# Attention output squares transposed on TensorE and summed on VectorE, and the second feed-forward bias added by GpSimd

## The chip, the cores and the metric

The kernel runs on one core of one Trainium2 chip. The metric is the device time in microseconds, taken from outside the program; the profiler's span runs from the first to the last instruction. Engines are named as in the profile: PE is TensorE's matmul stream and PEld its weight loads, DVE is VectorE, ACT is ScalarE, POOL is GpSimd, SP is SyncE.

## What is computed

A language-model tower of depth one over 32 sequences of 512 byte tokens with width 128. Six n-gram rows are gathered for each token from a table, scaled and summed, joined with a byte embedding, and projected (the embedding part). Three layers follow, each with an attention part and a feed-forward part. Last comes a mixture of eight experts, of which each token takes one (the routing part and the expert stage). What the change touches is inside a layer (cut to that):

```python
for l in range(LAYERS):
    Y = _msr(_layernorm(X, ln1_w[l], ln1_b[l]), ...) + X
    Hn = _layernorm(Y, ln2_w[l], ln2_b[l])
    X = gelu(Hn @ ffn_w1[l] + ffn_b1[l]) @ ffn_w2[l] + ffn_b2[l] + Y
# inside _msr, Y is the attention output by head, 32 numbers a head:
m = Y.mean(-1, keepdims=True)
v = ((Y - m) ** 2).mean(-1, keepdims=True)
Yn = ((Y - m) / sqrt(v + EPS)) * gnw + gnb
```

## The kernel before

**Streams and rounds.** Two sequences (s = 0, 1) are in work at a time, each cut into two halves of 256 tokens (h = 0, 1). So four streams run side by side, and each goes through three layers of `attend` and `feed`. A pair of sequences is one round of 12 half-layers, and there are 16 rounds (`pairs`). Beside the layers of round `it` run the embedding of round it+1 and the routing of the round before. The 48 table gathers of a round are indirect DMAs whose descriptors POOL makes; they lie in POOL's queue between its arithmetic, as filler that is due a round later. After the last round follows the expert stage, which the change does not touch.

**Order.** Every engine has one queue in program order. That order is made when the program is built: each part of a stream is a generator that yields a due time before each of its steps, from the tables `AT` and `FIRST_AT` (lines 50 to 171; one number for each stream and layer) and the stream's start, and `by_progress` (line 548) always takes the step with the smallest due time. So a step's due time sets its place in its engine's queue, and nothing is moved at run time: an engine that waits holds everything behind it. `LATER_GATHERS` (line 33) does the same for the gathers.

**The attention output.** The matmuls of `attend` (PE, lines 1565 to 1575) leave y transposed in PSUM: 128 features on the partitions, 256 tokens along the free axis. ACT writes its squares to `sq` (line 890) and y times `gn_w` to `zp` (line 891). PE multiplies each 128-token chunk of `sq` with a 128x4 matrix of heads (lines 1576 to 1581), which gives for each token the sum of squares of its four heads: 128x8 for a half. DVE scales that by 1/32, adds EPS and writes `ms` (lines 1257 to 1260). POOL raises it to the power -0.5 (`gr`, line 795). ACT spreads `gr` over the 32 features of a head (`xn`, line 896), PE transposes that (line 1584, "pe rT_y"), and DVE multiplies it into `zp` (lines 1263 and 1264). PE's `o` projection and DVE's residual `Y1` (line 1268) end the part. The V weights are centred by head in the setup, so y has mean zero over a head.

**The norms.** ACT sums the squares of `Y1` (line 859), POOL raises the sum to the power -0.5 (`rstd`, line 771, "pool rstd2"), ACT multiplies `Y1` with it into `xn` (line 865, "act xn2"), which signals `n_out`, and PE transposes `xn` ("pe norm2_T", line 1497). The norm ahead of an attention part goes the same way from `X` ("pool rstd1"), with DVE multiplying (line 1166).

**The feed-forward bias.** In `feed` PE accumulates hidden times W2 in PSUM and then adds the second bias with two bf16 matmuls of 129 columns (lines 1618 and 1619): `three_bf` has ones in its first three rows, and `bias2` holds the bias split in three bf16 parts, made in the setup by `split_bias2` (lines 1115 to 1130). DVE then writes X = PSUM + `Y1` (line 1277), having waited for `ff_p` (the PSUM result) and `y1_s` (`Y1` written).

PE's helper `mm` is line 1471, so most matmuls have that line; the groups are told apart by their tensors ("moving,stationary": `con,sq` is the mean-square matmul, `bias,three_bf` the bias matmul, `con,xn` a transpose by the identity). An f32 matmul shows as two instructions, a transpose as one.

Of the kernel before, what the change touches and what calls it, by code (L numbers as in the profile page):

```python
# [8 lines left out]
BF16 = mybir.dt.bfloat16  # L9
I32 = mybir.dt.int32  # L10
U32 = mybir.dt.uint32
ALU = mybir.AluOpType
# [37 lines left out]
AT = {  # L50
# [60 lines left out]
FIRST_AT = {  # L111
# [76 lines left out]
def columns(widths):  # L188
# [11 lines left out]
    ("region", E), ("half", 16), ("tile", 80), ("gram_row", NG),  # L200
# [10 lines left out]
def constants(n_tokens):  # L211
# [31 lines left out]
    c[:, CONST["half"]] = -0.5  # L243
    c[:, CONST["tile"]] = np.arange(80)
# [4 lines left out]
def tower_program(nc, x, gram_table, layer_w, params, consts, expert_w, out):  # L249
# [13 lines left out]
    with ExitStack() as ctx:  # L263
        def sb(name, shape, dt=F32):
            return ctx.enter_context(nc.sbuf_tensor(name, shape, dt))
# [4 lines left out]
        def two(make, name, *a):  # L270
            return [make(f"{name}{s}", *a) for s in range(2)]
# [25 lines left out]
        def param(name, k=None, width=1):  # L297
            a = par[:, PARAM[name]]
            return a if k is None else a[:, k * width:(k + 1) * width]
# [18 lines left out]
        bias2 = sb("bias2", [P, LAYERS * WIDE], BF16)  # L318
        bias2_part = [sb(f"bias2_part{n}", [P, LAYERS * WIDE], BF16) for n in range(3)]
        bias2_rest = sb("bias2_rest", [P, LAYERS * WIDE])  # L320
        three_bf = sb("three_bf", [P, P], BF16)
        below_three = sb("below_three", [P, 1])
# [93 lines left out]
        def chunks(ap):  # L416
            return ap.rearrange("p (c n) -> p c n", c=CH)
# [52 lines left out]
        y1_s = two(sem, "attention_residual_ready")  # L470
        f_p = two(sem, "ffn_hidden_in_psum")
# [135 lines left out]
        def bank_a(s, h):  # L607
            return bank(s, 2 * h)
# [82 lines left out]
        def _(pool):  # L691
# [76 lines left out]
            def norm_rstd(it, s, k, h):  # L768

                pool.wait_ge(n_ss[s][h], nth(it, OWN, k))  # L770
                pool.tensor_tensor(rstd[s][:, CS[h]], ss[s][:, CS[h]], const("half")[:, 0:2], ALU.pow)\  # L771
                    .then_inc(n_rstd[s][h], 1)
# [24 lines left out]
            def feed(it, s, l, h):  # L797
                yield at("pool rstd2", it, s, h, l)
                norm_rstd(it, s, 2 * l, h)

# [33 lines left out]
        def _(act):  # L834
# [38 lines left out]
            def attend(it, s, l, h):  # L873
# [16 lines left out]
                act.activation(sq[s][:, CS[h], :], chunks(bank_a(s, h))[:, 0:2, :], ACT.Square)  # L890
# [99 lines left out]
        def _(dve):  # L990
# [124 lines left out]
            def split_bias2():  # L1115

                rest = param("ffn_b2")
                for n in range(3):
                    link(dve.tensor_copy(bias2_part[n][:, :], rest))
                    if n < 2:  # L1120
                        link(dve.tensor_tensor(bias2_rest[:, :], rest, bias2_part[n][:, :], ALU.subtract))
                        rest = bias2_rest[:, :]
                link(dve.tensor_scalar(bias2[:, :], bias2_part[0][:, :], eye[:, 0:1], None, ALU.mult))
                for n in (1, 2):
                    link(dve.scalar_tensor_tensor(bias2[:, :], bias2_part[n][:, :], eye[:, n:n + 1], bias2[:, :],
                                                  ALU.mult, ALU.add))
                link(dve.tensor_scalar(below_three[:, :], const("vocab"), 3.0, None, ALU.is_lt))
                dve.tensor_scalar(three_bf[:, :], ones_bf[:, :], below_three[:, :], None, ALU.mult)

            split_bias2()  # L1130
# [84 lines left out]
            def attend(it, s, l, h):  # L1215
# [34 lines left out]
                for m in range(2):  # L1250
# [8 lines left out]
                dve.tensor_scalar(ms[s][:, h * n:(h + 1) * n], a[:, 2 * P:2 * P + n], 1.0 / HD, EPS, ALU.mult, ALU.add)\  # L1259
                   .then_inc(y_ms[s], 1)  # L1260
# [10 lines left out]
            def feed(it, s, l, h):  # L1271
                k = it * LAYERS + l
                cs = CS[h]
                yield at("dve x", it, s, h, l)
                dve.wait_ge(ff_p[s], nth(k, 2, h))
                dve.wait_ge(y1_s[s], nth(k, 2, h))
                dve.tensor_tensor(X[s][:, cs, 0:WIDE], wide(bank_a(s, h)), Y1[s][:, cs, 0:WIDE], ALU.add).then_inc(x_s[s], 1)
# [191 lines left out]
        def _(pe):  # L1469
# [50 lines left out]
            def attend(it, s, l, h):  # L1520
# [57 lines left out]
                for c in half_chunks(h):  # L1578
                    last = mm(a[:, 2 * P + c % 2 * HEADS:2 * P + (c % 2 + 1) * HEADS], sq[s][:, c, :],
                              const("heads").rearrange("p (n d) -> p n d", d=HD)[:, :, 0])  # L1580
                last.then_inc(ms_p[s], 1)
# [9 lines left out]
            def feed(it, s, l, h):  # L1591
# [20 lines left out]
                for f in range(FB):  # L1612
                    if f % 2 == 0:
                        yield at(f"pe w2_{f // 2}", it, s, h, l)
                        pe.wait_ge(f_s[s], nth(k, 4, 2 * h + f // 2))
                    for i in range(2):
                        mm(wide(a)[:, i, :], hid[s][:, h, f, chunk(i)], w2[:, f, :], f == 0 and i == 0, False)
                for i in range(2):
                    last = mm(wide(a)[:, i, :], three_bf[:, :], bias2[:, l * WIDE:(l + 1) * WIDE], False, i == 1)
# [135 lines left out]
```

## Time and profile before

| what | us |
|---|---|
| runs: median of 3 (lowest, highest) | 2427.72 (2426.78, 2428.72) |
| the profiled execution's own time | 2428.14 |
| its span | 2426.3 |
| PE busy over the span | 2233.4 (92%) |
| PEld busy | 1950.1 (80%) |
| DVE busy | 1887.8 (78%) |
| POOL busy | 1764.3 (73%) |
| ACT busy | 1580.5 (65%) |

The own time is 1.8 us above the span (what lies around the first and last instruction) and 0.4 us above the median of the runs. The span has three stretches: a head of some 100 us, in which the tables are loaded, hashed and gathered; the 16 rounds, to about 2200 us; and the expert stage. Busy shares are averages over all three, so a stage is read from windows and from the timeline. PE's matmuls overlap in the records; what one costs in a full queue is the distance between starts, not its duration. POOL's queue shows gaps of 0.2 to 0.3 us ahead of each indirect DMA (put down to "issue"), in which it isn't free either.

### The profile page before, as it was taken

How to read it: one execution, taken by the hardware profiler on the slowest of the kernel's cores; microseconds unless marked ns; L12 is line 12 of the kernel's file. 1: busy time of each engine (PE TensorE's matmuls, PEld its weight loads, DVE VectorE, ACT ScalarE, POOL GpSimd, SP SyncE). 2: the span in 40 equal slices, each digit the busy share in tenths (PEclk: the TensorE clock that was granted, in tenths of full speed). 3: DMA queues.
4: the chain of work that ended last, by engine and by line, in shares of the span. 5: the costliest groups of instructions: out<-in, count | busy, mean ns of one | idle time of the engine just before them, and what ended most of it. 6: DMA issues, size and time to landing. Idle time of an engine off the chain costs nothing.

```text
span 2426.3 us, 52865 instructions
## 1 busy us (share of the span) xinstructions
PE 2233.4 (92%) x18308; PEld 1950.1 (80%) x18309; DVE 1887.8 (78%) x5669; ACT 1580.5 (65%) x5066; POOL 1764.3 (73%) x1762
## 2 busy tenths in 40 slices
PE   1489999999999999999999999999999999986985
PEld 0368888888888888888888888888888888875874
DVE  5757878888787888888888888887878888766653
ACT  0256677776767676776776777767676777763653
POOL 5687777777777777777787777777777774333777
PEclk9789999999999999999999999999999999997997
DMA  3111111111111111111111111111111111002332
GB/s 122 28 45 34 24 41 28 40 29 41 27 40 28 36 32 37 33 35 37 26 43 26 42 27 40 29 41 27 37 30 37 33 28 55 2 8 75 101 103 69
DMA packets 63522, 98.11 MB, mean 40 GB/s; under 512 B 19108, under 2 KB 41126, under 8 KB 63152
## 3 DMA queue, kind: packets, MB, share of 16 engines
q0 software_dynamic: 33216, 67.44, 10.6%
q1 hardware_dynamic: 30064, 27.53, 4.1%
q8 instruction: 141, 2.31, 0.4%
q14 instruction: 101, 0.83, 0.1%
HBM read 76.63 MB, written 19.17 MB: 39 GB/s over the span
## 4 chain that ended last, share of the span: by engine, by line
PE 75%; POOL 9%; DVE 8%; issue 4%; ACT 3%; DMA 0%; DVEq 0%; POOLq 0%; SPq 0%
PE psum L1471 65%; PE psum L1492 7%; POOL both_grams L760 4%; PE psum L1545 3%; POOL gr L795 3%; POOL out L821 3%; DVE hid L1254 2%; ACT qm L885 1%; ACT qkT L883 1%; ACT xn L896 1%; DVE side_n L1205 1%; DVE qk L1233 0%; DVE hid L1230 0%; DVE qk L1229 0%; POOL rstd L771 0%
## 5 line engine op out<-in xcount | busy, mean ns | idle before, releaser
L760 POOL DMA_INDIRECT both_grams<-gram_table,idx_all x768 | 780.3, 1016 | 188.5 <-issue 183.0
L1471 PE MATMUL psum<-xT,lw 128*128 128x256 f32 x1920 | 481.8, 385 | 0.0
L795 POOL TENSOR_TENSOR gr<-ms,con 128x8 f32<-128x8 f32 x192 | 319.1, 1662 | 137.9 <-DVE ms L1259 133.1
L1471 PE MATMUL psum<-lw,hid 128*128 128x129 f32 x3072 | 391.0, 276 | 3.4 <-ACT hid L915 3.4
L1471 PEld LDWEIGHTS psum<-lw,hid 128*128 128x128 f32 x3072 | 370.9, 192 | 12.9 <-issue 5.6
L771 POOL TENSOR_TENSOR rstd<-ss,con 128x2 f32<-128x2 f32 x320 | 233.9, 733 | 195.1 <-ACT squares L859 192.7
L1471 PEld LDWEIGHTS psum<-xT,lw 128*128 128x128 f32 x1920 | 341.2, 192 | 32.5
L915 ACT ACTIVATE hid<-psum,par 128x256 f32<-128x256 f32 x768 | 307.1, 486 | 43.8 <-PE psum L1471 41.1
L1471 PE MATMUL psum<-lw,xT 128*128 128x256 f32 (+1 forms) x1536 | 287.9, 330 | 6.5 <-ACT xT L871 6.5
L871 ACT ACTIVATE xT<-psum,par 128x256 f32<-128x256 f32 x384 | 213.5, 560 | 119.8 <-PE psum L1492 118.8
L1471 PEld LDWEIGHTS psum<-lw,xT 128*128 128x128 f32 x1536 | 250.0, 192 | 33.0 <-ACT xT L871 7.2
L1254 DVE TENSOR_TENSOR hid<-psum,con 128x512 f32<-128x512 f32 x384 | 249.5, 684 | 27.2 <-PE psum L1471 23.9
L1492 PE MATMUL psum<-con,xn 128*128 128x128 f32 x1152 | 238.5, 289 | 32.0 <-ACT xn L896 16.4
L1471 PE MATMUL psum<-qm,qkT 64*128 64x256 f32 x1536 | 219.7, 405 | 28.9 <-ACT qm L885 17.2
L1492 PEld LDWEIGHTS psum<-con,xn 128*128 128x128 f32 x1152 | 130.6, 147 | 91.8 <-issue 27.1
L865 ACT ACTIVATE xn<-Y,rstd 128x128 f32<-128x128 f32 x384 | 133.0, 396 | 102.1 <-POOL rstd L771 102.1
L883 ACT ACTIVATE qkT<-psum 128x512 f32<-128x512 f32 x192 | 114.5, 596 | 108.9 <-PE psum L1545 107.2
L1471 PEld LDWEIGHTS psum<-qm,qkT 64*128 64x128 f32 x1536 | 133.3, 187 | 64.0 <-ACT qm L885 23.4
L1229 DVE TENSOR_TENSOR qk<-psum,con 128x512 f32<-128x512 f32 x192 | 131.6, 685 | 65.8 <-PE psum L1471 65.7
L859 ACT ACTIVATE squares<-Y 128x129 f32<-128x129 f32 x384 | 116.1, 308 | 97.1 <-DVE Y L1268 97.1
L1205 DVE SCALAR_TENSOR_TENSOR side_n<-both_grams,gate,side_n 128x256 f32<-128x256 f32 x320 | 157.2, 491 | 8.1
L885 ACT ACTIVATE qm<-psum,con 128x256 f32<-128x256 f32 x384 | 160.8, 477 | 0.0
(244 smaller groups left out, 4747.6 us busy)
## 6 DMA issues: line engine op xcount, KB each, us to landing
both_grams<-gram_table,idx_all POOLq DMA_INDIRECT x768
xb<-x SPq DMA_DIRECT2D x32, 256.0 KB, 3.3
idx_all<-routed_rows SPq DMA_DIRECT2D x20, 132.0 KB
er<-routed_rows SPq DMA_DIRECT2D x20, 132.0 KB
both_grams<-routed_rows SPq DMA_DIRECT2D x20, 132.0 KB
qm<-routed_rows SPq DMA_DIRECT2D x20, 132.0 KB
both_grams<-expert_w SPq DMA_DIRECT2D x8, 321.0 KB, 5.2
lw<-layer_w SPq DMA_DIRECT2D x1, 2503.5 KB, 11.9
```

Source lines behind the costliest of these rows:

```text
L760: pool.indirect_dma_start(grams[s][:, g, c, :], None, gram_table, bass.IndirectOffsetOnAxis(ap=idx_all[:, g, at:at + 1], axis=0))\
L771: pool.tensor_tensor(rstd[s][:, CS[h]], ss[s][:, CS[h]], const("half")[:, 0:2], ALU.pow)\
L795: pool.tensor_tensor(gr[s][:, c], ms[s][:, c], const("half")[:, 0:n], ALU.pow).then_inc(y_r[s], 1)
L865: last = act.activation(xn[s][:, c, :], src[s][:, c, 1:WIDE], ACT.Copy, scale=scale[s][:, c:c + 1])
L871: act.activation(xT[s][:, TS[h]], src[:, 0:2 * P], ACT.Identity, bias=b, scale=w).then_inc(xT_s[s][h], 1)
L883: act.activation(qkT[s][:, h].rearrange("p a c n -> p (a c n)"), bank_b(s, h), ACT.Copy)
L885: last = act.activation(qm[s][:, h, j, :], bank_b(s, h)[:, 0:2 * P], ACT.Copy, scale=const("parity")[:, j:j + 1])
L915: last = act.activation(hid[s][:, h, 2 * m + f, :], src[:, f * 2 * P:(f + 1) * 2 * P], ACT.Gelu, bias=param("ffn_b1", l * FB + 2 * m + f))
L1205: last = dve.scalar_tensor_tensor(acc, grams[s][:, g, CS[h], :], gate[:, g:g + 1], acc, ALU.mult, ALU.add)
L1254: dve.tensor_tensor(A[s][:, h, m], chunks((a, b)[m]), causal.unsqueeze(1).to_broadcast([P, HEADS, P]), ALU.mult).then_inc(sc_s[s], 1)
L1471: return pe.matmul(dst, lhsT, rhs, start=start, stop=stop)
L1492: last = pe.transpose(dst[:, (c % 2) * P:(c % 2 + 1) * P], src[:, c, :], eye)
```

## The change

It has two parts. **The squares.** ACT's square takes a scale of 32^-0.5 and a bias of (EPS/32)^0.5, a new constant column, so that the sum of 32 squares is the mean square plus EPS (the cross term vanishes, since y has mean zero over a head). PE transposes the two chunks of `sq` into 256 PSUM columns where it had multiplied them with the heads, and DVE sums them by head, 32 at a time, with a `tensor_reduce` of 128x256 to 128x8 where it had scaled 128x8. **The bias.** The two bf16 matmuls of each half-layer go, and with them the setup that splits the bias. POOL adds the f32 bias to `Y1` in place, 128x258 numbers, in a step of its own, "pool bias", due at 7.2 us in `feed` for every stream and layer. It waits for `n_out` (ACT has read `Y1` for the norm), and DVE's X waits for the semaphore `y1_b` of that step in place of `y1_s`.

```diff
 AT = {
+    "pool bias": ((7.2, 7.2, 7.2), (7.2, 7.2, 7.2), (7.2, 7.2, 7.2), (7.2, 7.2, 7.2)),
...
 FIRST_AT = {
+    "pool bias": ((7.2, 7.2, 7.2), (7.2, 7.2, 7.2), (7.2, 7.2, 7.2), (7.2, 7.2, 7.2)),
...
-    ("region", E), ("half", 16), ("tile", 80), ("gram_row", NG),
+    ("region", E), ("half", 16), ("root_eps", 1), ("tile", 80), ("gram_row", NG),
...
+    c[:, CONST["root_eps"]] = (EPS / HD) ** 0.5
...
-        bias2 = sb("bias2", [P, LAYERS * WIDE], BF16)
...
             def feed(it, s, l, h):
                 yield at("pool rstd2", it, s, h, l)
                 norm_rstd(it, s, 2 * l, h)
+                yield at("pool bias", it, s, h, l)
+                pool.wait_ge(n_out[s][h], nth(it, NORMS, 2 * l + 1))
+                pool.tensor_tensor(Y1[s][:, CS[h], 0:WIDE], Y1[s][:, CS[h], 0:WIDE],
+                                   param("ffn_b2", l, WIDE).unsqueeze(1).to_broadcast([P, 2, WIDE]), ALU.add)\
+                    .then_inc(y1_b[s], 1)
...
-                act.activation(sq[s][:, CS[h], :], chunks(bank_a(s, h))[:, 0:2, :], ACT.Square)
+                act.activation(sq[s][:, CS[h], :], chunks(bank_a(s, h))[:, 0:2, :], ACT.Square,
+                               bias=const("root_eps"), scale=float(HD) ** -0.5)
...
-            def split_bias2():
...
-            split_bias2()
...
-                dve.tensor_scalar(ms[s][:, h * n:(h + 1) * n], a[:, 2 * P:2 * P + n], 1.0 / HD, EPS, ALU.mult, ALU.add)\
-                   .then_inc(y_ms[s], 1)
+                dve.tensor_reduce(ms[s][:, h * n:(h + 1) * n], a[:, 2 * P:].rearrange("p (n d) -> p n d", d=HD),
+                                  axis=AX_X, op=ALU.add).then_inc(y_ms[s], 1)
...
-                dve.wait_ge(y1_s[s], nth(k, 2, h))
+                dve.wait_ge(y1_b[s], nth(k, 2, h))
...
-                for c in half_chunks(h):
-                    last = mm(a[:, 2 * P + c % 2 * HEADS:2 * P + (c % 2 + 1) * HEADS], sq[s][:, c, :],
-                              const("heads").rearrange("p (n d) -> p n d", d=HD)[:, :, 0])
-                last.then_inc(ms_p[s], 1)
+                half_transposes(a[:, 2 * P:], sq[s], h).then_inc(ms_p[s], 1)
...
-                        mm(wide(a)[:, i, :], hid[s][:, h, f, chunk(i)], w2[:, f, :], f == 0 and i == 0, False)
-                for i in range(2):
-                    last = mm(wide(a)[:, i, :], three_bf[:, :], bias2[:, l * WIDE:(l + 1) * WIDE], False, i == 1)
+                        last = mm(wide(a)[:, i, :], hid[s][:, h, f, chunk(i)], w2[:, f, :], f == 0 and i == 0,
+                                  f == FB - 1 and i == 1)
                 last.then_inc(ff_p[s], 1)
```

## Rows read from the trace of the kernel before

**Rows 1.** the page, part 4, whole span: engines on the chain that ended last

```profile
PE 75%; POOL 9%; DVE 8%; issue 4%; ACT 3%; DMA 0%; DVEq 0%; POOLq 0%; SPq 0%
```

**Rows 2.** windows, 900 to 1300 us: length, then busy us per engine, PE clock, DMA

```profile
900.00:1300.00 400.00, 395.43 (x3342) 345.96 (x3341) 331.75 (x988) 284.50 (x932) 311.69 (x311) 1.00 0.13 34
```

**Rows 3.** POOL timeline, one round apart: start, us, instruction, [idle before]

```profile
942.58 1.65 POOL L795 TENSOR_TENSOR gr<-ms,con 128x8 f32<-128x8 f32 x1
...
1071.74 1.65 POOL L795 TENSOR_TENSOR gr<-ms,con 128x8 f32<-128x8 f32 x1
```

**Rows 4.** groups by line and form, whole span: count, busy us, mean ns, idle

```profile
L1259 DVE TENSOR_SCALAR ms<-psum 128x8 f32<-128x8 f32 x192 | 31.9, 166 | 40.8 <-PE psum L1471 40.8
...
L1263 DVE TENSOR_TENSOR zp<-psum,zp 128x256 f32<-128x256 f32 x192 | 80.5, 419 | 28.1 <-PE psum L1492 26.2
```

**Rows 5.** PE timeline, two stretches of a middle round

```profile
910.31 0.50 PE L1471 MATMUL psum<-con,sq 128*128 128x4 f32 x4
910.68 0.41 PE L1492 MATMUL psum<-con,xn 128*128 128x128 f32 x2
...
919.64 0.28 PE L1471 MATMUL psum<-bias,three_bf 128*128 128x129 bf16 x2
919.76 0.39 PE L1492 MATMUL psum<-con,xn 128*128 128x128 f32 x2
919.98 0.51 PE L1471 MATMUL psum<-par,side_T 128*128 128x8 f32 x4
```

**Rows 6.** DVE timeline, setup

```profile
28.32 0.29 DVE L1109 TENSOR_REDUCE lw<-lw 128x1 f32<-128x128 f32 x1
...
29.16 0.69 DVE L1109 TENSOR_REDUCE lw<-lw 128x4 f32<-128x512 f32 x1
...
35.73 0.35 DVE L1201 TENSOR_SCALAR side_n<-both_grams,gate 128x256 f32<-128x256 f32 x1 [3.87 <-DMA both_grams<-gram_table,idx_all]
```

**Rows 7.** POOL timeline, setup: one integer sum of 48 and one of 720 numbers

```profile
14.15 0.28 POOL L719 TENSOR_TENSOR hid<-hid 128x48 int32<-128x48 int32 x1
...
87.40 1.70 POOL L719 TENSOR_TENSOR rest_limb<-rest_limb,qm 128x720 int32<-128x720 int32 x1
```

**Rows 8.** DVE timeline at 87 us, and line 1205: ns min/median/max

```profile
87.51 4.22 DVE L1205 SCALAR_TENSOR_TENSOR side_n<-both_grams,gate,side_n 128x256 f32<-128x256 f32 x3
...
L1205 DVE SCALAR_TENSOR_TENSOR side_n<-both_grams,gate,side_n x320: 468/485/1862, 36.1 to 2021.9; 128x256 f32<-128x256 f32 x160
```

**Rows 9.** waits of POOL, 500 to 1800 us: us in total, times, longest

```profile
POOL rstd L771 <- ACT squares L859: 82.2, 128, 1.5
...
POOL gr L795 <- DVE ms L1259: 63.8, 51, 1.9
```

**Rows 10.** POOL timeline of a middle round, four of its chained powers

```profile
907.90 0.70 POOL L771 TENSOR_TENSOR rstd<-ss,con 128x2 f32<-128x2 f32 x1 [0.57 <-ACT squares L859]
...
911.20 1.69 POOL L795 TENSOR_TENSOR gr<-ms,con 128x8 f32<-128x8 f32 x1
...
919.75 0.86 POOL L771 TENSOR_TENSOR rstd<-ss,con 128x2 f32<-128x2 f32 x1 [0.38 <-ACT squares L859]
...
951.91 0.73 POOL L771 TENSOR_TENSOR rstd<-ss,con 128x2 f32<-128x2 f32 x1
```

**Rows 11.** ACT timeline, the normalisation after the power at 919.75

```profile
920.64 0.69 ACT L865 ACTIVATE xn<-Y,rstd 128x128 f32<-128x128 f32 x2 [0.98 <-POOL rstd L771]
```

**Rows 12.** PE timeline, transposes that those results feed, and the scores behind

```profile
921.49 0.44 PE L1492 MATMUL psum<-con,xn 128*128 128x128 f32 x2
...
944.83 0.38 PE L1492 MATMUL psum<-con,xn 128*128 128x128 f32 x2
...
945.94 1.14 PE L1471 MATMUL psum<-qm,qkT 64*128 64x256 f32 x8 [0.29 <-ACT qm L885]
...
953.50 0.38 PE L1492 MATMUL psum<-con,xn 128*128 128x128 f32 x2
```

**Rows 13.** chain of waits, 100 to 240 us (the first round): shares by line

```profile
by line: POOL both_grams L760 31.6%; PE psum L1471 25.4%; issue 10.0%; POOL gr L795 7.4%; POOL rstd L771 5.2%; PE psum L1492 3.2%; PE psum L1545 1.3%; DVE X L1182 1.1%; ACT hid L915 1.1%; DVE lw L1111 1.0%; DVE hid L1254 0.9%; ACT L915 0.9%
```

More of the change, by code:

```diff
@@ L317, in tower_program @@
         Y1 = two(sb, "Y1", [P, CH, WIDE + 1])
-        bias2 = sb("bias2", [P, LAYERS * WIDE], BF16)
[L319 to L322, printed above, removed]
         xn = two(sb, "xn", [P, CH, H])
@@ L470, in tower_program @@
         y1_s = two(sem, "attention_residual_ready")
+        y1_b = two(sem, "attention_residual_with_bias_ready")
         f_p = two(sem, "ffn_hidden_in_psum")
@@ L1113, in _ @@
             centred(param("ffn_b2").rearrange("p (l n) -> p l n", l=LAYERS))
-            def split_bias2():
[L1117 to L1128, printed above, removed]
-            split_bias2()
             for s in range(2):
```

## The prediction

> **What bounds the kernel now.** I read the chain of waits first: PE holds 75% of it, POOL 9%, DVE 8% [rows 1]. Then a window in the middle: of 400 us PE is busy 395, at granted clock 1.00 (the 2.4 GHz level), DVE 332, POOL 312 [rows 2]. The timeline repeats itself: the same `gr` starts at 942.58 and at 1071.74, so a round is 129.2 us [rows 3], and 14 of the 16 rounds are alike. PE's queue is full; its starts follow each other without gaps. But the other queues are close behind. POOL waits on semaphores only 82.2 + 63.8 = 146 us in 1300 us, ten rounds, so 14.5 us a round [rows 9]; in the other 114.7 it works or issues DMAs. Where PE's next input comes from POOL's power (`rstd`, `gr`), its margin is small, and that decides this change.
>
> **PE, removed and added.** The mean-square group starts at 910.31 and the next at 910.68: 0.37. A pair of transposes takes 919.76 to 919.98: 0.22. The two bias matmuls take 919.64 to 919.76: 0.12 [rows 5]. So PE saves 0.15 + 0.12 = 0.27 in each of the 192 half-layers, 3.2 us a round, 52 us in all. Were PE the only limit, 2428 would become 2376, and no edit here can give more.
>
> A transpose takes 0.11 for 128 columns [rows 5] in a stretch at clock 1.00 [rows 2], with hundreds of transposes in it. The Trainium skill (TensorE: Matmul & The Clock Gate, Part 4: PE-mode transpose) says that transposes do not bring the clock to its full rate. By that rule a pair would cost an estimated 0.44, PE would lose 0.07 instead of gaining 0.15, and the sum below would end some 20 us higher. The rows here speak against it, and it gets no chance.
>
> **DVE.** `ms` takes 0.17 on 8 numbers; a DVE operation that reads 256 PSUM numbers takes 0.42 [rows 4]. Sums of 128 and 512 numbers take 0.29 and 0.69 [rows 6], which puts 256 at 0.42 too. Bounds 0.29 and 0.69; I take 0.42. That is 0.25 more per half-layer, 3.0 a round, on an engine that is busy 83% [rows 2]. On the path from PE's squares to `gr` it is 0.25 - 0.15 = +0.1. ACT's square with a scale and a bias keeps its shape; I cost it at nothing, since ACT has a quarter of its time free [rows 2].
>
> **POOL's new step.** No f32 sum on POOL is in the trace. The nearest are integer sums: 0.28 for 48 numbers and 1.70 for 720 [rows 7]; a line through them gives 0.72 for 258. Bounds: 0.28 (all fixed cost) and 1.70; in practice 0.4 to 0.85. I take 0.72. It adds 12 x 0.72 = 8.6 us a round against 14.5 of waiting, so POOL still fits into a round (about 123 of 126 to 129), but with most of its slack gone. What counts is where in the queue it falls. I merged the due times of the tables as the program does:
>
> Place 1: two bias steps fall between the power at 907.90 and the one at 919.75, the first right behind 907.90, the second one step behind `gr` at 911.20. POOL waited only 0.38 ahead of 919.75 [rows 10], so that power comes 2 x 0.72 - 0.38 = 1.06 late. ACT normalises from 920.64 for 0.69 [rows 11] and PE's transposes start at 921.49 [rows 12], 0.16 after it; some 0.1 of that is spare. PE stalls about 0.95.
> Place 2: a bias step falls directly ahead of the power at 951.91, which already followed POOL's queue without a wait [rows 10]. It ends 0.86 before PE's transposes at 953.50 [rows 12], and the same normalisation lies between. PE stalls 0.66.
> Place 3: a bias step falls one gather ahead of `gr` at 942.58, which had no wait ahead of it [rows 3]. It ends at 944.23, its transposes start at 944.83, and the scores at 945.94 waited 0.29 for ACT [rows 12], which works behind the spreading of `gr`. PE stalls 0.72.
> The other eight fall ahead of waits that take them, or of results whose margin is larger. With the +0.1 of the sums at some three `gr` that start when `ms` arrives, a round gains stalls of 0.95 + 0.66 + 0.72 + 0.3 = 2.6.
>
> Against that stands PE's saving, but where PE waits for such a result, what it saved since it fed that path is lost in the wait. By the same merging some 4 bias groups and 6 squares groups of a round lie in such stretches: 4 x 0.12 + 6 x 0.15 = 1.4. So 3.2 - 1.4 = 1.8 is kept, and a round grows by 2.6 - 1.8 = 0.8.
>
> **Waits and setup.** POOL's wait for `n_out` holds its queue, but the norm is applied some 2 us or more before the bias is reached, so it costs nothing; DVE's X is due at 10.68 at the earliest against 7.2 for the bias, so `y1_b` comes about 3 us ahead, and if that cover went, X and the next layer of that stream would be late by what is missing. No DMA moves to another queue, but every gather behind a bias step is issued later; they are due a round ahead, which hides it. The setup that goes (ten DVE steps before 28 us) lies ahead of a 3.87 us wait of DVE for the first gathers [rows 6]: nothing gained.
>
> **The sum.** 14 rounds x 0.8 = +11. In the first round POOL itself is the chain: gathers 31.6, `gr` 7.4, `rstd` 5.2, issue 10.0, together 54% [rows 13]; 12 x 0.72 x 0.54 = +4.7. In the last round there are no gathers, POOL has room, and PE keeps 3.2 - 0.6 = -2.6. Together +13 on the profiled execution's own 2428.14 (0.4 above the median of the runs): 2441 us.
>
> **Rivals.** A, faster: POOL's add is short. With its duration d the stalls of the three places are 4d - 0.54; against 1.8 - 0.3 kept they break even at d = 0.51. At d = 0.28, the fixed cost of the row, they are 0.6, and about half of the lost savings come back (0.6): a round shrinks by 1.5, 14 x 1.5 + 2.6 - 2 = 22, so 2406; with all savings kept some 2390. For it: PE's full queue and its 75% of the chain. Against it: the slope of the integer sums. The case d = 0.45 to 0.6 is the one of no change.
> B, slower still: POOL's add holds up DVE. While the sum of 720 ran on POOL (87.40 for 1.70 [rows 7]), three DVE operations with two SBUF inputs took 4.22 us, where the median of one is 0.485 and the longest took 1.862 [rows 8], so DVE stood until POOL's sum was done. The Trainium skill (SBUF — State Buffer, SBUF: two separate sides) says that the two engines share one port pair that is locked for a whole instruction; the trace agrees. Here, a DVE operation that meets a bias step would stand for half of it on average, 0.36. If half of the 12 meet one in a stretch where DVE has no wait to give, that is 2.2 a round, 14 x 2.2 = 30, and 2471; if all do, 2500. Against it: DVE still has 17% free, and the small powers of POOL show no such stand.
>
> **Chances.** Forecast (POOL late at three places, 2441, by itself 2433 to 2458) 0.40; B (2471) 0.20; A (2390 to 2422) 0.27; no change 0.13. A measurement of this kernel can tell about 0.2%, 5 us. That gives faster 0.27, same 0.13, slower 0.60. The range must reach into A and B: 2395 leaves out the end of A, 2488 the end of B, together under 2 in 10.
>
> **What would show it.** Right: mean-square transposes 0.22 apart, no bias matmuls, `ms` near 0.42, POOL's new add near 0.72; a round of about 130; POOL's waits for ACT's squares and DVE's `ms` down from 14.5 to some 6 a round; PE waits for ACT's normalisation at the three places. Wrong: an add under 0.5 with rounds below 129 (A); DVE operations with two SBUF inputs far above their medians and PE waiting for DVE (B); X waiting for the bias, which I cost at nothing; or new waits at other places, since the margins come from one order of events.

## The result and the profile after

The changed kernel takes 2506.33 us (median of 5 runs, 2504.79 to 2507.31), the kernel before 2427.72 beside it: a ratio of 1.0324, interval 1.0313 to 1.0336, 78.6 us slower. The prediction was 2441 with a range to 2488: the side was right, the size was not.

First the chain that ended last, part 4 of the page of the kernel after (shares of the span, by engine, then by line):

```profile
POOL 42%; DVE 25%; PE 19%; issue 10%; ACT 4%; DMA 0%; DVEq 0%; POOLq 0%; SPq 0%
PE psum L1460 16%; POOL both_grams L759 15%; POOL gr L794 9%; POOL rstd L770 5%; POOL routed_rows L812 5%; DVE hid L1243 4%; POOL Y L801 3%; POOL out L825 2%; DVE qk L1222 2%; PE psum L1481 2%; ACT squares L863 2%; DVE hid L1219 2%; DVE qk L1218 2%; DVE side_n L1194 1%; DVE ms L1248 1%
```

Before, PE held 75% of it [rows 1]; now POOL does most, and the new add itself (L801) is only 3%. Another engine has become the bound, and not by the new step alone: by all that stands in the same queue. The window of [rows 2], after (busy us of each engine, granted clock):

```profile
900.00:1300.00 400.00, 376.83 (x3069) 318.88 (x3068) 337.85 (x950) 273.96 (x890) 326.61 (x333) 1.00 0.12 33
```

PE went from 395 to 377 of 400 at the same clock of 1.00, POOL from 312 to 327. The round, from the timeline of POOL after (start, duration): the same bias add one round apart.

```profile
903.73 0.90 POOL L801 TENSOR_TENSOR Y<-Y,par 128x258 f32<-128x258 f32 x1
...
1038.83 0.91 POOL L801 TENSOR_TENSOR Y<-Y,par 128x258 f32<-128x258 f32 x1
```

135.1 us, against 129.2 [rows 3]. 14 rounds of 5.9 would be 83 us, a little over the 78.6, since some rounds after take 134.7; so nearly all of the loss is in the steady rounds. The terms of the sum, from the instructions grouped by form after (busy us, mean ns, idle time before them); the first row is of the whole span, the other two of 500 to 1800 us:

```profile
L801 POOL TENSOR_TENSOR Y<-Y,par 128x258 f32<-128x258 f32 x192 | 144.9, 755 | 3.2 <-ACT xn L869 0.8
...
L1248 DVE TENSOR_REDUCE ms<-psum 128x8 f32<-128x256 f32 x116 | 48.3, 417 | 9.0 <-PE psum L1481 9.0
...
L894 ACT ACTIVATE sq<-psum,con 128x256 f32<-128x256 f32 x116 | 54.2, 468 | 13.2 <-PE psum L1460 12.7
```

and a pair of mean-square transposes with what follows it, in the timeline of PE after:

```profile
896.25 0.38 PE L1481 MATMUL psum<-con,sq 128*128 128x128 f32 x2
896.50 1.99 PE L1460 MATMUL psum<-xT,lw 128*128 128x256 f32 x8
```

The add (0.755 against 0.72 taken), the sum (0.417 against 0.42) and the pair (0.25 here, against 0.22) came out near the terms; the square, costed at nothing, takes 468 ns where it took 378. The add waited 0.8 us for `n_out` in the whole run. Now the waits from 500 to 1800 us after (us in total, times, longest); 1300 us are 9.6 rounds:

```profile
ACT xn L901 <- POOL gr L794: 66.0, 87, 1.4
...
POOL gr L794 <- DVE ms L1248: 58.7, 59, 2.4
...
POOL rstd L770 <- ACT squares L863: 50.2, 88, 1.5
DVE xn L1155 <- POOL rstd L770: 43.3, 47, 1.4
...
PE psum L1481 <- ACT xn L901: 23.7, 38, 0.9
...
DVE X L1171 <- POOL side_mom L775: 19.5, 20, 1.7
...
PE psum L1481 <- ACT xn L869: 18.8, 29, 1.2
...
DVE xn L1155 <- POOL rstd L783: 13.4, 10, 1.4
PE psum L1534 <- DVE qk L1222: 13.3, 29, 0.6
```

and of before, all waits of DVE for POOL's powers and all waits of PE (10.1 rounds):

```profile
DVE xn L1166 <- POOL rstd L771: 24.2, 30, 1.2
...
PE psum L1471 <- ACT qm L885: 10.4, 20, 0.7
...
DVE X L1182 <- POOL side_mom L776: 2.6, 10, 0.3
...
PE psum L1471 <- DVE hid L1254: 2.2, 10, 0.2
```

POOL still waits 109 us, 11.3 a round, where it waited 14.5 [rows 9]. So of the 9.1 us that 12 adds bring to a round only 3.2 went into its waits, and the other 5.9 are the growth of the round. DVE waits 76 us for powers of POOL, 7.9 a round, where it waited 26.8 us, 2.7 a round. These waits stand in DVE's queue, ahead of work for all four streams. Nothing waited for the add itself or for a gather in that stretch.

PE's matmuls (the weight loads, PEld, not counted) waited 12.6 us before, 1.3 a round, and never for `xn`. After, all its waits come to 69.8 us, 7.3 a round. The three places of the prediction are among them, in the timeline of PE after (place 1, 3 and 2):

```profile
953.31 0.44 PE L1481 MATMUL psum<-con,xn 128*128 128x128 f32 x2 [1.21 <-ACT xn L869]
...
977.83 0.44 PE L1481 MATMUL psum<-con,xn 128*128 128x128 f32 x2 [0.93 <-ACT xn L901]
...
987.07 0.44 PE L1481 MATMUL psum<-con,xn 128*128 128x128 f32 x2 [0.45 <-ACT xn L869]
```

They are 2.6 us together, against 0.95 + 0.66 + 0.72 = 2.3 forecast. The other 3.4 us a round that were added stand where the sum has no price but 0.3 for the squares' sums, such as 0.81 for `xn` at 934.96 and 0.60 for DVE's rotary sum at 915.94. A stretch of the chain after, in order of time (start, us, what), shows how POOL's lateness travels through DVE's queue:

```profile
910.67 0.74 POOL side_mom L775
911.41 0.03 issue
911.44 0.04 DVE X L1171
...
915.20 0.69 DVE qk L1222
915.89 0.33 DVE sw L1226
916.22 0.34 DVE ms L1248
916.57 0.07 issue
916.63 1.63 POOL gr L794
...
1005.89 1.67 POOL gr L794
...
1027.77 0.72 POOL rstd L770
```

and the waits in it, from the timelines: first the same X of DVE before, then X and `gr` after.

```profile
880.50 0.67 DVE L1182 TENSOR_SCALAR X<-h,side_mom 128x128 f32<-128x128 f32 x2 [0.26 <-POOL side_mom L776]
...
911.44 0.66 DVE L1171 TENSOR_SCALAR X<-h,side_mom 128x128 f32<-128x128 f32 x2 [1.71 <-POOL side_mom L775]
...
916.63 1.63 POOL L794 TENSOR_TENSOR gr<-ms,con 128x8 f32<-128x8 f32 x1 [0.16 <-DVE ms L1248]
```

Here the waiting runs in a loop. POOL comes late to a power, behind two of the new adds; DVE's X (of the side stream) waits 1.71 us for it at the head of DVE's queue, where it waited 0.26; the DVE operations behind it start late one after the other, the last of them is `ms`, and POOL, late as it is, still waits for that `ms` at `gr`. Such a wait is no room: it moves with POOL. How many of POOL's waits are of this kind no view adds up; e5 and e13 measure it from outside. From 1005.89 to 1027.77 POOL works and issues without one wait.

### The profile page after: what moved, and what is told of

It is laid out like the page before. It is cut to its first block, busy times and chain, and to the rows that moved or that the text cites. A ratio compares the mean times of both kernels' runs of the same rounds, so it can differ in the third digit from the quotient of the medians.

```text
span 2504.9 us, 51511 instructions
## 1 busy us (share of the span) xinstructions
PE 2223.9 (89%) x17540; PEld 1888.7 (75%) x17541; DVE 1972.8 (79%) x5659; ACT 1595.9 (64%) x5066; POOL 1914.7 (76%) x1954
## 4 chain that ended last, share of the span: by engine, by line
POOL 42%; DVE 25%; PE 19%; issue 10%; ACT 4%; DMA 0%; DVEq 0%; POOLq 0%; SPq 0%
PE psum L1460 16%; POOL both_grams L759 15%; POOL gr L794 9%; POOL rstd L770 5%; POOL routed_rows L812 5%; DVE hid L1243 4%; POOL Y L801 3%; POOL out L825 2%; DVE qk L1222 2%; PE psum L1481 2%; ACT squares L863 2%; DVE hid L1219 2%; DVE qk L1218 2%; DVE side_n L1194 1%; DVE ms L1248 1%
## 5 line engine op out<-in xcount | busy, mean ns | idle before, releaser
L759 POOL DMA_INDIRECT both_grams<-gram_table,idx_all x768 | 789.6, 1028 | 178.9 <-issue 173.6
L1481 PEld LDWEIGHTS psum<-con,xn 128*128 128x128 f32 x1152 | 128.3, 144 | 188.9 <-ACT xn L901 78.3
L812 POOL DMA_INDIRECT routed_rows<-row,slot x128 | 137.5, 1074 | 36.4 <-issue 32.9
```

Of the source, the lines that this page charges most:

```text
L759: pool.indirect_dma_start(grams[s][:, g, c, :], None, gram_table, bass.IndirectOffsetOnAxis(ap=idx_all[:, g, at:at + 1], axis=0))\
L812: pool.indirect_dma_start(slots, bass.IndirectOffsetOnAxis(ap=slot[s][:, c:c + 1], axis=0), row[s][:, c, :], None).then_inc(r_done[s], 16)
L1481: last = pe.transpose(dst[:, (c % 2) * P:(c % 2 + 1) * P], src[:, c, :], eye)
```

## The experiments

Theory Q: GpSimd's queue lost the time. Rivals: VectorE's longer sums (D), the add holding VectorE up by its memory access (L), and others that each expectation names. The kernel before took 2427.2 to 2427.9 beside each group of runs, so times of different groups can be set against each other. The first four runs split the change.

**e1, the squares alone**

```diff
-  act.activation(sq, y, ACT.Square)
+  act.activation(sq, y, ACT.Square, bias=const("root_eps"), scale=HD ** -0.5)
-  dve.tensor_scalar(ms, a[:, 2P:2P+n], 1/HD, EPS, mult, add)
+  dve.tensor_reduce(ms, a[:, 2P:] by heads, add)
-  mm(..., sq, const("heads")) twice
+  half_transposes(a[:, 2P:], sq, h)
```

> Only the squares part is made; the bias stays on PE. Theory Q (POOL's new step in its queue is the whole cost): PE saves 0.15 in each half-layer, DVE's sum is 0.25 longer but covered, so 2400 to 2430 us. Theory D (the longer path from the squares to the power: DVE 0.17 to 0.42, ACT 0.38 to 0.47) : at least 50 of the 79 us, 2475 or more. Theory X (neither alone, the two parts take each other's slack): 2430 to 2455.

Measured 2432.32, ratio 1.0020 (1.0011 to 1.0029): a small loss, just past Q's range, inside that of X, and far from D.

**e2, the bias alone** (the rest of the diff: GpSimd's add, no bias matmuls)

> Only the bias part is made; the squares go through the matmul with the heads as before. Theory Q: most of the 79 us, 2480 to 2510. Theory D: 2415 to 2440, since PE loses 0.12 of work in each half-layer and POOL has room. Theory X: 2435 to 2460, less than half of the loss.

2505.72, ratio 1.0324 (1.0310 to 1.0338): the whole loss, within 0.6 us of the full change. It lies in Q's range; D and X fall.

**e3, squares with the bias left out altogether**, and **e4, the kernel before with the bias left out**

```diff
-  pool.tensor_tensor(Y1, Y1, ffn_b2, add).then_inc(y1_b)      # and no bias matmuls
-  dve.wait_ge(y1_b)
+  dve.wait_ge(y1_s)
```

> The changed kernel without POOL's step; the second feed-forward bias is left out of the computation altogether, so PE has neither its matmuls nor POOL its sum. Theory Q: PE's whole saving of up to 52 us shows, 2380 to 2405. Theory D: still slower than before, 2450 or more. Theory X: between 2405 and 2440.

> The kernel before without its two bias matmuls; the second feed-forward bias is left out of the computation. It prices the PE work alone: 192 x 0.12 = 23 us if PE is the only limit, 2405; near 2427 if other queues take it up. All three theories expect 2405 to 2420; Theory X expects the upper end.

2418.46 (0.9965, 0.9952 to 0.9978) and 2413.36 (0.9944, 0.9929 to 0.9960). e4 lies in the range that all had, e3 above Q's, in that of X: TensorE's whole saving did not show, and here Q was wrong. Taking the bias off TensorE is worth 14 of the 23 us that 192 x 0.12 make, and the squares cost 5 us with or without it. GpSimd's step costs 2505.7 - 2413.4 = 92 us for 144 us of work. All later costs are counted from e4.

**e5, a power of the same length in place of the add; bias left out**

```diff
-  pool.tensor_tensor(Y1, Y1, ffn_b2, add).then_inc(y1_b)
+  pool.tensor_tensor(spare, const("rank")[:, 0:2], const("half")[:, 0:2], pow).then_inc(y1_b)
```

> The squares as in the kernel before; GpSimd's step stands at its place, waits and signals as in the bias-only kernel, but it is a power of 128x2 values from constants into a scratch tile, so it has nearly the duration of the add (the other 128x2 powers take 0.70 to 0.74 us, the add 0.755) and touches 4 columns of a partition instead of 774. The second feed-forward bias is left out of the result. Theory Q (GpSimd's queue is the resource: each step of 0.7 us makes the powers behind it late, and VectorE and ScalarE wait in order for those): what counts is the duration, so 2485 to 2510 us, nearly the 2505.7 of the bias-only kernel. Rival L (the add and VectorE hold each other up when both read and write wide tiles): the power takes that away, so at most half of the 92 us stays, 2413 to 2460. Rival W (VectorE's sum waits for GpSimd's signal): that needs only the place and the signal, as Q, but then VectorE's X would show idle time behind this step.

2481.19, ratio 1.0220 (1.0206 to 1.0234), 67.8 over e4: between the two, much nearer to Q. A step that reads 4 numbers a partition and helps nobody costs 73% of what the add costs, by standing in the queue. W falls, since no instruction waited for the step. For the other 24 us the groups by form of DVE, 500 to 1800 us, first of e5:

```profile
L1252 DVE SCALAR_TENSOR_TENSOR zp<-zp,par,sw 128x256 f32<-128x256 f32 x116 | 57.3, 494 | 4.1
...
L1337 DVE TENSOR_TENSOR pick_bf<-picked,top 128x16 bf16<-128x16 f32 x40 | 7.7, 193 | 1.4
```

then of e2, with the add:

```profile
L1252 DVE SCALAR_TENSOR_TENSOR zp<-zp,par,sw 128x256 f32<-128x256 f32 x115 | 65.1, 566 | 4.1
...
L1337 DVE TENSOR_TENSOR pick_bf<-picked,top 128x16 bf16<-128x16 f32 x39 | 12.8, 328 | 1.3
```

The same instructions are longer with the add: 566 against 494 ns, 328 against 193. Of the 115 `zp` in e2, the 28 that ran beside an add took 526 to 1056 ns, 806 on average, and the others 489. About 4 of the 24 us are due to length, since the add takes 749 ns and this power 731 (at the 200 us for each us that e13 gives). By the window 900 to 1300, DVE's busy time times the round over 400 is 107 us a round before, in e4 and in e5, and 111 in e2.

**e6, half of the add; the other chunk's bias left out**

```diff
+  first = slice(2 * h, 2 * h + 1)
-  pool.tensor_tensor(Y1[:, CS[h]], Y1[:, CS[h]], ffn_b2 twice, add)
+  pool.tensor_tensor(Y1[:, first], Y1[:, first], ffn_b2, add)
```

> As the bias-only kernel, but GpSimd adds the bias to the first of a half's two token chunks alone (128x129 values instead of 128x258), at the same place and with the same wait and signal; the other chunk's bias is left out of the result. It should take some 0.4 to 0.5 us instead of 0.755. The kernel without the step takes 2413.4 us and the one with it 2505.7. Theory Q with a queue that is full at this place: the cost follows the step's whole length on GpSimd, so 92 x (0.4 to 0.5)/0.755 = 49 to 61, 2460 to 2475 us. Rival S (GpSimd has some slack a round, and the cost starts when that is used up): less than in proportion, 2420 to 2450. Rival F (the step costs by being there, a wait and a signal in the queue, not by its length): over 2480.

2455.11, ratio 1.0112 (1.0096 to 1.0127), 41.7 over e4 for a step of 451 ns: between Q and S, F falls.

**e7, the same add at other places in GpSimd's queue**

```diff
- "pool bias": ((7.2, 7.2, 7.2), (7.2, 7.2, 7.2), (7.2, 7.2, 7.2), (7.2, 7.2, 7.2)),
+ "pool bias": ((7.2, 4.4, 10.4), (3.95, 8.25, 11.85), (7.2, 7.2, 10.95), (4.0, 7.2, 5.15)),
```

> The bias-only kernel with nothing changed but due times of GpSimd's step: of a round's 12 steps 8 are put directly ahead of a power at which GpSimd waited in the trace of the kernel without the step (for the mean squares from VectorE or the sums from ScalarE, 0.27 to 1.72 us each, 6.6 us in all), the other 4 stay. The result is complete. Theory Q: what lies in a wait costs nothing, so the part of the 8 steps beyond their waits (about 1.2 us a round) and the 4 others (3 us) are left of 9 us a round: a third to a half of the 92, 2440 to 2465 us. Rival L (the add holds VectorE up by its reads and writes wherever it stands): 2490 to 2510. Rival C (a wait of GpSimd is closed by the time that it was itself late earlier, so a step in it only moves it): 2475 to 2500.

2470.13, ratio 1.0175 (1.0161 to 1.0189). It lies between Q and C: 36 of the 92 us are had back by places alone, but 57 stay. The waits of POOL in e7, 500 to 1800 us:

```profile
POOL rstd L770 <- ACT squares L863: 39.4, 59, 1.5
POOL gr L794 <- DVE ms L1247: 33.7, 33, 2.1
...
POOL Y L801 <- ACT xn L869: 8.0, 10, 0.8
```

That is 8.3 us in each of 9.8 rounds, where e2 has 11.4 and e4, without the step, 13.7: at these places 5.4 us of waiting were filled, at the old ones 2.3. So the places count. What the 57 us are made of this run does not tell. Four steps were not moved, and 14 rounds of 4 x 0.73 are 41 us if each costs its length; one moved step waits 0.8 us a round for `n_out`; and the add still holds VectorE up. That a step in a wait of the loop costs something is therefore not shown here.

**e8, the squares-only kernel without scale and bias operand; both left out of the result**

```diff
-  act.activation(sq, y, ACT.Square, bias=const("root_eps"), scale=HD ** -0.5)
+  act.activation(sq, y, ACT.Square)
```

> The squares-only kernel (bias by TensorE as before, squares transposed and summed by VectorE), but ScalarE's square has no scale and no bias operand, as in the kernel before: the division by the head size and the epsilon are left out of the result. ScalarE's square should take 378 ns again instead of 469. The squares-only kernel takes 2432.3 us, 5 above before, and I had expected a gain of some tens of us. Theory A (ScalarE's 0.09 us a half-layer, on the way from the attention output to the powers, took part of the gain): 192 x 0.09 = 17 us at most, 2415 to 2427 us. Rival V (VectorE's sum, 0.25 us longer than the copy that it replaces and on the same way, took it): 2430 to 2434, no change. Rival N (TensorE's saving was never on the way): also no change.

2429.84, ratio 1.0009 (1.0000 to 1.0018), with the square back at 378 ns: 2.5 us less than e1, which is less than the 0.2% that a measurement can tell, so 0.09 us in each of 192 steps counts for little. A falls; N and V are left.

**e9, the squares-only kernel with half of the sum; the other half of the squares left out**

```diff
-  dve.tensor_reduce(ms, a[:, 2P:] by heads, add)
+  dve.tensor_reduce(ms, (a[:, 2P:] by heads)[:, :, 0:HD // 2], add)
```

> The squares-only kernel, but VectorE's sum takes the first half of each head's values alone (128x128 read instead of 128x256); the other half of the squares is left out of the result. VectorE's sum should take about 0.29 us (as its other 128x128 from PSUM) instead of 0.42. The squares-only kernel takes 2432.3 us. Theory V (VectorE's longer step on the way from the attention output to GpSimd's power is what takes the gain of TensorE): half of the 0.25 us more goes, 192 x 0.13 = 25 us at most, 2410 to 2425. Rival N (VectorE has idle time here and TensorE's saving was never on the way, so neither counts): 2428 to 2434.

2421.66, ratio 0.9974 (0.9964 to 0.9985). The group of the sum in e9, 500 to 1800 us:

```profile
L1261 DVE TENSOR_REDUCE ms<-psum 128x8 f32<-128x128 f32 x121 | 34.7, 287 | 14.4 <-PE psum L1494 14.0
```

0.13 us less per sum gave 10.6 of 25 us: V, and N falls. VectorE's longer step is what the squares part pays, and TensorE's 0.15 does not outweigh it. Whether it pays on the way to `gr` or by holding the rest of VectorE's queue, this run does not separate.

**e10, a shorter power in the kernel before; the powers of six of a half's eight values left out**

```diff
-  pool.tensor_tensor(gr[8 columns], ms[8 columns], const("half")[:, 0:8], pow)
+  pool.tensor_tensor(gr[2 columns], ms[2 columns], const("half")[:, 0:2], pow)
-  act.activation(xn by heads, gr[8 columns] spread over 32 each, Copy)
+  act.activation(xn, gr[2 columns] spread over 128 each, Copy)
```

> The kernel before, but GpSimd's power of the mean squares takes 2 of a half's 8 values a partition (128x2 instead of 128x8), and ScalarE spreads these two over all heads; the powers of the other heads are left out of the result. This step should take 0.72 us instead of 1.69, 0.97 less, 12 times a round. The runs so far gave 92.6 us for each 1 us that was put into GpSimd's queue per half-layer step (power instead of the add: 67.8 for 0.731; half add: 41.7 for 0.451). Theory Q2 (GpSimd's queue already sets the round in the kernel before, and the cost is a straight line through it): the same slope downwards, 0.97 x 92.6 = 90 us less, 2335 to 2350 us. Rival K (TensorE sets the round before, as 395 of 400 us busy say, and the queue's cost only begins there: a knee at about the time of the kernel without the bias): 2410 to 2427 us. Rival M (shorter latency helps in part): 2370 to 2405.

2415.65, ratio 0.9947 (0.9933 to 0.9960). The row of e10 in the window 900 to 1300:

```profile
900.00:1300.00 400.00, 396.16 (x3355) 347.44 (x3348) 331.55 (x986) 284.58 (x932) 279.15 (x312) 1.00 0.13 34
```

K, and Q2 and M fall: GpSimd lost 33 of 312 us and the kernel 12 us in all. PE stayed at 396 of 400. Before the change the queue did not set the round.

**e11, the same add on VectorE**

```diff
-  pool.wait_ge(n_out); pool.tensor_tensor(Y1, Y1, ffn_b2, add).then_inc(y1_b)
+  dve.wait_ge(n_out);  link(dve.tensor_tensor(Y1, Y1, ffn_b2, add))
```

> The bias-only kernel with the same in-place add at the same due time, issued by VectorE instead of GpSimd, with no signal to wait for at X. The result is complete. VectorE is busy for 107 of a round's 128.3 us without the step; its other 128x258 adds take 0.42 us, so 5 us a round more. Theory Q (it is GpSimd's queue that is short of time, not VectorE's): VectorE has room, and a step costs its length where something waits behind it, at the 0.48 that GpSimd's showed or less: 192 x 0.42 x 0.48 = 39 us over the kernel without the step, 2425 to 2455 us. Rival V (VectorE has in-order waits of its own and every us counts in full): 2413 + 81, 2485 to 2500 us. Rival F (VectorE's step is free, as it lies in its idle time): 2411 to 2420 us, faster than before.

2431.15, ratio 1.0014 (1.0005 to 1.0023): 18 us over e4, in Q's range, where GpSimd's step costs 92. Its group and the chain of e11:

```profile
L1258 DVE TENSOR_TENSOR Y<-Y,par 128x258 f32<-128x258 f32 x192 | 80.4, 419 | 0.0
```

```profile
PE 61%; DVE 21%; POOL 9%; issue 6%; ACT 2%; DMA 0%; DVEq 0%; POOLq 0%; SPq 0%
```

VectorE is busier than GpSimd by the busy row, and still had the room: its 80 us of work cost 18, it adds nothing to GpSimd's queue with the 44 powers and 56 DMA issues of a round, and PE stays on the chain.

**e12, the bias matmuls of the kernel before as one**

```diff
-  for i in range(2): mm(wide(a)[:, i, :], three_bf, bias2[l], False, i == 1)
+  mm(wide(a), three_bf, bias2[l] twice, False, True)
```

> The kernel before, but TensorE adds the bias to a half's two chunks by one multiplication of 258 columns instead of two of 129. The result is complete. In the trace of the kernel before the pair takes 0.12 us from its start to the next start at a clock of 1.00 (0.06 each). If TensorE pays by columns alone: no change, within 0.2% of before. If each instruction has a cost of its own that the neighbours don't hide: up to 0.03 us less each, 192 x 0.03 = 6 us at most, 2421 to 2426.

2424.93, ratio 0.9990 (0.9981 to 0.9999). The timeline of PE in e12:

```profile
906.24 0.27 PE L1471 MATMUL psum<-bias,three_bf 128*128 128x258 bf16 x1
906.35 0.38 PE L1492 MATMUL psum<-con,xn 128*128 128x128 f32 x2
```

0.11 to the next start instead of 0.12 [rows 5]. It is the fastest version with a complete result, by less than the 0.2% that a measurement can tell, so the two theories are not told apart.

**e13, a still shorter power in the queue; bias left out**

```diff
-  pool.tensor_tensor(spare[2 columns], const("rank")[:, 0:2], const("half")[:, 0:2], pow)
+  pool.tensor_tensor(spare[1 column], const("rank")[:, 0:1], const("half")[:, 0:1], pow)
```

> The kernel with a power in place of the add, but the power takes 1 value a partition instead of 2 (128x1). The second feed-forward bias is left out of the result. The powers of 128x2 and 128x8 took 0.73 and 1.70 us, 0.16 for each value more, so this one should take about 0.57. The same place, wait and signal. Straight line (the queue's cost starts with the first ns: 67.8 us for 0.731): 0.57 x 92.7 = 53 us over the 2413.4 of the kernel without the step, 2463 to 2470. Slack first (the half add's 41.7 hold some 10 us of hold-up of VectorE, so the queue's part is 31 for 0.451 and 68 for 0.731, 130 us for each us behind a slack of 0.2): 47 us, 2456 to 2462. Present at all (the step costs by its being there): over 2475.

2455.20, ratio 1.0113 (1.0097 to 1.0130), 41.8 over e4. The groups of the two powers, e13 first:

```profile
L802 POOL TENSOR_TENSOR spare<-con 128x1 f32<-128x1 f32 x192 | 115.3, 601 | 3.2 <-ACT xn L869 0.8
```

```profile
L802 POOL TENSOR_TENSOR spare<-con 128x2 f32<-128x2 f32 x192 | 140.4, 731 | 3.1 <-ACT xn L869 0.8
```

The duration was 0.601, not 0.57, and the time is still below both ranges: the line is steeper than either theory had it. 0.13 us more in each of 192 steps cost 26 us, and 192 x 0.13 is 25: between these two lengths the queue's time counts in full. Followed down, the cost ends at 0.601 - 41.8/200 = 0.39 us a step, 4.7 us a round. An estimate from two points, but the waits of POOL from 500 to 1800 us bear it out, in e4:

```profile
POOL rstd L769 <- ACT squares L857: 74.2, 119, 1.5
POOL gr L793 <- DVE ms L1241: 64.4, 53, 2.0
```

and in e5:

```profile
POOL rstd L771 <- ACT squares L863: 53.1, 89, 1.5
POOL gr L795 <- DVE ms L1247: 37.6, 40, 2.1
```

138.6 us in 10.1 rounds of 128.3 are 13.7 a round; 90.7 in 9.8 rounds of 133.2 are 9.3. So at these places 4.4 us a round were filled, and 9.3 stayed although the rounds grew by 4.9.

**e14, e7 with the power in place of the add; bias left out**

```diff
- "pool bias": ((7.2, 7.2, 7.2), (7.2, 7.2, 7.2), (7.2, 7.2, 7.2), (7.2, 7.2, 7.2)),
+ "pool bias": ((7.2, 4.4, 10.4), (3.95, 8.25, 11.85), (7.2, 7.2, 10.95), (4.0, 7.2, 5.15)),
-  pool.tensor_tensor(Y1, Y1, ffn_b2, add).then_inc(y1_b)
+  pool.tensor_tensor(spare, const("rank")[:, 0:2], const("half")[:, 0:2], pow).then_inc(y1_b)
```

> The kernel with the steps moved ahead of GpSimd's waits, with the power of 128x2 constants in place of the add; the second feed-forward bias is left out of the result. With the add the moved steps gave 2470.1 us, 57 over the kernel without the step. Hold-up (the add stops VectorE when both want wide tiles): VectorE's busy time a round was 2.4 us longer with the moved add than with a power, against 3.9 for the add at its first place, which cost 24 us more than the power; so 24 x 2.4/3.9 = 15 us less, 2450 to 2460 us. No hold-up (the 24 came from the order of events of that one pair): 2466 to 2472. Moving alone decides (what stands in a wait is free): the 4 steps that stay and what sticks out of the waits, some 25 us, 2435 to 2445.

2457.88, ratio 1.0125 (1.0108 to 1.0142): 12.3 us below e7, 44.5 over e4, in the range of the hold-up, although the power took longer here (777 ns against 728 for the moved add). So the hold-up shows in a second pair, 12 us beside the 24. Moving alone falls (2435 to 2445).

## Why the prediction was right or wrong

**The account.** From e2, e4 and e5: +68 for the time in GpSimd's queue, +24 for what only the add does, -14 for the bias matmuls, +78 together, and the full change is 0.6 us above that. The squares cost 5 us alone and nothing measurable beside the bias, since PE is then no longer the bound.

**PE's saving.** Its size was right, its worth was not. The bias matmuls gave 14 of 23 us (e4), about the share that I let PE keep. The squares gave less than nothing (e1), because VectorE's step between the attention output and `gr` became longer (e9). I had that as 0.25 - 0.15 = +0.1 at some three `gr`, and it was more: half of the sum's growth is worth 10.6 us (e9). The square's 0.09, costed at nothing "since ACT has a quarter of its time free", lies on the same way, but e8 gives it 2.5 us, within what a measurement can tell.

**The failed step** is "The other eight fall ahead of waits that take them, or of results whose margin is larger", and with it the sum of 2.6 us of stalls and the round of +0.8. The three stalls that were priced came: 2.6 us, against 2.3. But PE's waits grew by 6.0 us a round, so 3.4 us stand where the sum has 0.3 and the other eight steps were to cost nothing; and since the round grew by 5.9, next to nothing of the 1.8 us that PE was to keep is seen. Two things broke the step. First, POOL's 14.5 us of waiting [rows 9] were taken as room for 8.6. In the changed kernel they shrank by 3.2, and the power in place of the add filled 4.4 (e5). The chain after shows why for one of them: it is a wait for DVE, which had itself waited for POOL. That most of the rest are of this kind is inferred from their staying, not shown one by one, and the room depends on the places (5.4 in e7). Second, I followed POOL's lateness to PE at the powers' direct users only, with everything else left where it was, and not into DVE's queue, where `xn` and the side stream's X wait in order for powers, 7.9 us a round after, with the masks, the rotary products and `ms` behind them. "POOL still fits into a round" was the wrong test: a queue with some 4.5 us to give at these places was given 9.

**Rival A** fell on its own condition: the add took 0.755, over the 0.51 of the break-even.

**Rival B**, the add holding up DVE, was real but was the smaller part: 24 us of the 92 (e2 against e5) and 12 in the second pair (e7 against e14), where its text said 30. DVE's busy time grew by 4 us a round, nearly the 0.36 x 12 = 4.3 of "if all do"; that this cost 24 us and not 14 x 4 = 56 suggests that over half of it fell where DVE would have waited. The Trainium skill (SBUF — State Buffer, SBUF: two separate sides) says that a GpSimd instruction that reads SBUF and a VectorE operation with two SBUF inputs lock each other out for a whole instruction. For the wide add the trace agrees that VectorE is held (`zp` beside an add 806 ns, else 489). For GpSimd's small powers it does not: the 40 `zp` of e5, 500 to 1800 us, that ran beside a power took 483 to 486 ns; the measurement decides.

**Signs that were named.** Right: the add near 0.72, the sum near 0.42, the pair of transposes, X not waiting for POOL's add, PE's waits at the three places. Wrong: a round of 130 (135.1) and POOL's waits "down to some 6 a round" (11.3). The sign that was named last, new waits at other places, came. Waits that stay while the round grows are what a loop would give.

**Open:** the half add costs 41.7 us at 0.451 us. By the line of e13 its time in the queue would be 0.06 x 200 = 12, which leaves 30 to the hold-up, more than the whole add's 24. DVE's busy time grew by only 1.9 us a round there, so this was not explained. The half add and the power of e5 lie on one line through nothing (93 us for each us of a step), and e13 lies 14 us below that line; so how the cost grows with the length, and with it the 0.39 us, rests on few points. Nor does a run tell which of the eight moved steps of e7 found real room.

## What to carry to other kernels

Before work is put into an engine's waiting time, ask what each wait waits for: where that thing waited, some steps earlier, for the same engine, the wait is a loop's and will be there again after the engine has become later. The room is what can be filled until the loop closes (here some 4.5 of 14 us a round at the places of the change, 5.4 at those of e7), and past it the queue's time costs (here, from 0.60 to 0.73 us a step, a us for each us). An engine that only issues small powers and DMAs can be nearer to that point than one with a higher busy share: the same add cost 92 us on GpSimd, at 0.75 us a step, and 18 on VectorE, at 0.42.

## What the runs showed of the hardware

- ScalarE's square of 128x256 from PSUM took 378 ns, and 468 with a bias operand and a scale; in e8, without both, 378 again. The Trainium skill (ScalarE: Activation LUTs, What ACT_TABLE_LOAD costs) says that each per-partition pointer operand adds about 93 ns; the trace agrees, with 90.
- GpSimd's add of 128x258 f32 with two SBUF inputs took 728 to 755 ns on average (e7, after) and half of it 451 (e6), VectorE's same add 419 (e11). A power took 0.60 us for 1 value a partition (e13), 0.73 to 0.78 for 2 (e5, e14) and 1.66 for 8 (before), though it touches almost nothing.
- VectorE's `zp` with two SBUF inputs took 526 to 1056 ns beside GpSimd's wide add (e2) and 483 to 486 beside a power (e5).
- One bf16 multiplication of 258 columns took 0.11 us to the next start, two of 129 took 0.12, at a granted clock of 1.00.
